# Attention and FFN block on one core: the value products of a step's two query blocks interleaved

## The chip, the cores and the metric

The kernel runs on one core of a Trainium2 chip. The metric is the device time of one execution in microseconds (us); lower is better. PE is TensorE, PEld its weight loads, DVE is VectorE, ACT is ScalarE, POOL is GpSimd, SP is SyncE, which here only issues DMAs.

## The reference, cut to what matters

One transformer layer on x of 1 x 2048 x 128 in fp32: layer norm, attention of 16 heads of 8 dimensions in a causal window of 32 tokens, a residual, layer norm, and a feed-forward part of 512 hidden units with GELU and a small weight update, again with a residual.

```python
scores = jnp.einsum('bhqd,bhkd->bhqk', q, k) * scale
allowed = (j <= i) & (i - j < WINDOW)          # WINDOW = 32
scores = jnp.where(allowed, scores, NEG_INF)
attn = jax.nn.softmax(scores, axis=-1)
out = jnp.einsum('bhqk,bhkd->bhqd', attn, v)   # the value products
...
x = x + attention(layernorm(x)); x = x + ffn(layernorm(x))
```

## The kernel before, in words

The 2048 tokens are cut into 8 chunks of 256, a chunk into 8 query blocks of 32 tokens (`WIN`). A block's queries see the keys of the block before and of their own, so each block has two windows `w` of 32 keys. The 16 heads form 4 groups (`NG`) of 4 (`GH`); a group's four heads stand one above the other in the 128 partitions, so one matmul serves four heads.

A **step** treats two blocks (`UB` = 2), so a chunk is 4 steps and the kernel has 32, numbered k here. Two chunks make a turn of 8 steps, and there are 4 turns, the middle ones in a hardware loop. The order on each engine is written out by hand in a function `step`; engines meet only at semaphores. On PE, step s does in this order:

1. `centre(s-1)` (L469): two bf16 matmuls of 512 columns that take the row maximum off the scores of step s-1, in PSUM.
2. `values(s-3)` (L490): the value products of step s-3.
3. `out_proj` (L536) in odd steps, `turn_att` (L532, a transpose of the attention output) in even ones.
4. In some steps pieces of a later chunk: `turn_x` (L416), `project` (L422, L423) and, behind the scores, `project_v` (L428).
5. `scores(s+1)` (L458): 16 bf16 matmuls, into the bank of scores that step s-1 used.

The bank of scores is double, so `scores(s+1)` waits until ACT has taken the exponential of step s-1 (`softmax_exp`, L684), which itself waits for `centre(s-1)`. DVE takes the maximum (L827), splits it (L833) and transposes the probabilities (L840), one step or more ahead of their use. All of ACT's copies share line L628 and are told apart by their tiles. ACT also copies the transposed attention output (attT), spreads the value rows out per head (V, 8 small copies at a time), copies xT for the next projection and in the last turn makes the token pairs of the FFN's weight update. Like every engine it works through its list in order.

In `values` each of a step's two blocks i has 4 groups x 2 windows = 8 fp32 products, each 32 stationary columns (the transposed probabilities) by 36 moving columns (the value rows of four heads and four columns of ones for the denominators). The result of block j stands in PSUM partitions 32q to 32q+31 with q = j mod 4, that is, in one of four 32-column tiles of the array. In a step the two blocks have q = 0 and 1, or q = 2 and 3. The two windows of a group are summed in PSUM (`start` at w = 0, `stop` at w = 1). The last product raises `pv_ps`, for which DVE and ACT wait. The program has 16 products in a step, and the trace shows each as two weight loads and two matmuls, as it does with every fp32 matmul: 32 matmul records in a step, 1024 in all.

After the last turn the FFN (`up` L513, `turn_x2` L499, `down` L611) runs with PE as the engine that never rests.

Of the kernel before, what the change touches and what calls it, by code (L numbers as in the profile page):

```python
# [26 lines left out]
P = 128  # L27
# [3 lines left out]
NG = HEADS // GH  # L31
WIN = 32
# [4 lines left out]
UB = BLOCKS // UNITS  # L37
# [13 lines left out]
def block_kernel(nc, x, Wq, bq, Wk, bk, Wv, bv, Wo, bo, W1, b1, W2, b2, scale, out):  # L51
# [10 lines left out]
    with ExitStack() as ctx:  # L62
# [112 lines left out]
        def ge(eng, s, value):  # L175

            if not isinstance(value, int) or value > 0:
                eng.wait_ge(s, value)
# [222 lines left out]
        def _(pe):  # L401
# [72 lines left out]
            def values(turn, s):  # L474
                k, b, u = SU * turn + s, s // UNITS, s % UNITS
                if u == 0:
                    c = 2 * turn + b
                    pe.wait_ge(v_done, c + 1)
                if isinstance(turn, int) and k == 0:
                    pe.wait_ge(wT_sb, 2)  # L480
                if s % 2 == 0:
                    ge(pe, att_done, (SU // 2) * turn + s // 2 - 1)
                pe.wait_ge(probsT_done, k + 1)
                o = bank_o[(s // 2) % 2]
                for i in range(UB):
                    j = UB * u + i
                    q = j % (P // WIN)
                    for g in range(NG):
                        for w in range(2):
                            mm = nc.tensor.matmul(o[q * WIN:(q + 1) * WIN, g * VC:(g + 1) * VC],  # L490
                                                  probsT[s % 2][:, i, g, w, :], V[b][:, j + w, g, :],
                                                  start=(w == 0), stop=(w == 1))
                mm.then_inc(pv_ps, 1)
# [44 lines left out]
            def step(turn, s, last):  # L538
# [7 lines left out]
                if not (first and s < 3) and s < SU + 3:  # L546
                    values(turn if s >= 3 else turn - 1, (s - 3) % SU)
# [463 lines left out]
```

## Time and profile before

| | |
|---|---|
| median of 3 runs | 165.35 us (164.3 to 165.49) |
| the profiled execution, first to last instruction | 162.8 us |
| mean granted TensorE clock | 0.979 |
| PE busy | 145.1 us, 89% of the span |
| PEld busy | 113.8 us, 70% |
| DVE busy | 99.5 us, 61% |
| ACT busy | 89.3 us, 55% |
| POOL busy | 51.0 us, 31% |
| `values` (L490), PE | 1024 matmuls, union of their records 36.8 us |
| `scores` (L458), PE | 512 matmuls, union 35.8 us |

The span is one execution seen by the profiler; the device time has some 2.5 us around it. Busy time of PE is a union of records whose ends are modelled: matmuls are pipelined, a record of L490 lasts 0.2 us while a new one starts every few hundredths, so for PE the distance between starts is what to read. "Granted clock" 1.00 is 2.4 GHz, 0.50 is 1.2 GHz.

### The profile page before, as it was taken

What the parts mean: (1) busy time and instruction counts of PE and PEld (TensorE: products, weight loads), DVE (VectorE), ACT (ScalarE), POOL (GpSimd) and SP (SyncE); (2) the same over time, 40 slices, a digit from 0 to 9 for tenths busy, and PEclk for the clock granted to TensorE, in tenths of its full rate; (3) what the DMA queues carried; (4) which work ended last, traced back from release to release, by engine and by line L of the source; (5) the groups of instructions that cost most, each with busy time, mean ns of one, the idle gap of its engine ahead of it and who ended that gap; (6) DMA issues with size and microseconds to landing.
All of it is one profiled execution on the core that took longest, in us unless ns stands there. A gap on an engine that the chain in (4) does not pass through costs nothing.

```text
span 162.8 us, 5053 instructions
## 1 busy us (share of the span) xinstructions
PE 145.1 (89%) x1923; PEld 113.8 (70%) x1923; DVE 99.5 (61%) x281; ACT 89.3 (55%) x256; POOL 51.0 (31%) x78
## 2 busy tenths in 40 slices
PE   0755298699999999999999999999799999999993
PEld 0423185578887887888788878788667665958792
DVE  6687956945576685695595597869665354221021
ACT  3354357558386577666677757529912567060600
POOL 6369578910060060051041030503600039800000
PEclk9999999659999999999999999999999999999999
DMA  1786897957044928618809908900000000020213
GB/s 50 219 215 243 202 366 168 330 168 178 0 151 167 240 97 268 188 61 297 195 4 332 212 0 306 230 19 0 4 0 4 0 2 4 0 64 0 64 45 88
DMA packets 27313, 21.10 MB, mean 130 GB/s; under 512 B 1304, under 2 KB 23071, under 8 KB 27295
## 3 DMA queue, kind: packets, MB, share of 16 engines
q1 hardware_dynamic: 27294, 20.85, 43.0%
q8 instruction: 12, 0.20, 0.5%
q14 instruction: 7, 0.05, 0.1%
HBM read 10.88 MB, written 9.96 MB: 128 GB/s over the span
## 4 chain that ended last, share of the span: by engine, by line
PE 80%; ACT 7%; DVE 5%; issue 2%; SPq 2%; DMA 1%; POOL 1%; DVEq 0%
PE bank_o L490 20%; PE bank_s L458 16%; PE bank_s L469 9%; PE bank_qk L611 4%; PE bank_s L513 4%; PE bank_w L536 3%; PE bank_v L611 3%; PE bank_o L513 3%; PE bank_qk L422 3%; ACT V L628 3%; PE bank_v L428 3%; PE bank_w L532 2%; PE bank_qk L423 2%; PE bank_t L416 2%; DMA x_sb<-in_L_attn_x_dram 1%
## 5 line engine op out<-in xcount | busy, mean ns | idle before, releaser
L490 PEld LDWEIGHTS bank_o<-V,probsT 128*32 128x32 f32 x1024 | 33.1, 114 | 15.1 <-issue 14.2
L458 PEld LDWEIGHTS bank_s<-KS,QS 128*128 128x128 bf16 x512 | 35.6, 166 | 4.5 <-ACT probs L684 3.9
L458 PE MATMUL bank_s<-KS,QS 128*128 128x64 bf16 x512 | 35.8, 225 | 2.3 <-ACT probs L684 2.2
L490 PE MATMUL bank_o<-V,probsT 128*32 128x36 f32 x1024 | 36.8, 201 | 0.0
L827 DVE TENSOR_REDUCE negmax<-bank_s 128x8 f32<-128x512 f32 x32 | 22.1, 690 | 22.9 <-PE bank_s L458 21.5
L684 ACT ACTIVATE probs<-bank_s 128x512 f32<-128x512 f32 x32 | 19.1, 598 | 22.4 <-PE bank_s L469 22.3
L628 ACT ACTIVATE V<-bank_v 32x64 f32<-32x64 f32 x128 | 27.5, 215 | 1.5
L840 DVE STREAM_TRANSPOSE probsT<-probs 128x512 f32<-128x512 f32 x32 | 22.5, 702 | 0.0
L285 POOL TENSOR_TENSOR q_parts<-rest,q_parts 128x256 bf16<-128x256 f32 x8 | 5.6, 705 | 53.7 <-ACT q_parts L628 53.7
L372 POOL TENSOR_TENSOR rstd<-var,half 128x4 f32<-128x4 f32 x4 | 4.1, 1020 | 28.6 <-DVE var L871 28.6
L469 PE MATMUL bank_s<-negmax,ident_bf 128*128 128x512 bf16 x32 | 12.6, 395 | 0.1
L469 PE MATMUL bank_s<-negmax_low,ident_bf 128*128 128x512 bf16 x32 | 12.6, 395 | 0.0
L628 ACT ACTIVATE attT<-bank_w,bias_cols 128x128 f32<-128x128 f32 x16 | 5.9, 369 | 11.4 <-PE bank_w L532 11.4
L833 DVE TENSOR_TENSOR negmax_low<-negmax 128x8 bf16<-128x8 f32 x32 | 11.3, 352 | 0.2
L416 PE MATMUL bank_t<-ident,xn 128*128 128x128 f32 x16 | 4.0, 342 | 7.0 <-DVE xn L800 7.0
L862 DVE TENSOR_TENSOR x<-bank_w,x_bo 128x128 f32<-128x128 f32 (+1 forms) x16 | 4.6, 286 | 9.1 <-PE bank_w L536 9.0
L628 ACT ACTIVATE q_parts<-bank_qk,bias_cols 128x256 bf16<-128x256 f32 x8 | 3.8, 475 | 10.4 <-PE bank_qk L423 10.4
L757 ACT ACTIVATE hidden<-bank_o,bias_cols 128x512 f32<-128x512 f32 x6 | 4.0, 687 | 8.7 <-PE bank_o L513 8.5
L416 PEld LDWEIGHTS bank_t<-ident,xn 128*128 128x128 f32 x16 | 2.1, 165 | 8.5 <-DVE xn L800 8.5
L270 POOL TENSOR_TENSOR rstd<-var,half 128x2 f32<-128x2 f32 (+2 forms) x4 | 6.0, 1493 | 6.1 <-DVE var L794 6.1
L422 PE MATMUL bank_qk<-xT,wq 128*128 128x256 f32 x16 | 6.7, 512 | 1.2 <-ACT xT L628 1.2
L611 PEld LDWEIGHTS bank_qk<-w2T,hidden 128*128 128x128 f32 x64 | 7.4, 192 | 0.5 <-issue 0.5
(109 smaller groups left out, 232.5 us busy)
## 6 DMA issues: line engine op xcount, KB each, us to landing
k_scr<-k_parts SPq DMA_DIRECT2D x8, 576.0 KB, 5.0
KS<-k_scr SPq DMA_DIRECT2D x8, 576.0 KB, 5.1
q_scr<-q_parts SPq DMA_DIRECT2D x8, 512.0 KB, 3.0
QS<-q_scr SPq DMA_DIRECT2D x32, 128.0 KB, 3.0
x_sb<-in_L_attn_x_dram SPq DMA_DIRECT2D x1, 768.0 KB, 5.3
out_dram<-y SPq DMA_DIRECT2D x3, 256.0 KB, 2.3
w<-in_L_ffn_W_dram SPq DMA_DIRECT2D x2, 256.0 KB, 5.4
x_sb<-in_L_attn_x_dram SPq DMA_DIRECT2D x2, 128.0 KB, 2.2
```

Of the source, the lines that this page charges most:

```text
L416: mm = nc.tensor.transpose(bank_t[:, t * P:(t + 1) * P], xn[b][:, t], ident[:])
L422: nc.tensor.matmul(bank_qk[:, 0:CHUNK], wq[:], xT[b][:], start=True, stop=True)
L458: mm = nc.tensor.matmul(dst, QS[b][:, o, g].rearrange("p h t -> p (h t)")[:, j::BLOCKS], KS[b][:, o, g, j * WIN:(j + 2) * WIN], start=(i = ...
L469: mm = nc.tensor.matmul(bank_s[s % 2][:].rearrange("p (a k) -> p a k", k=2 * WIN), ident_bf[:], part.unsqueeze(2).to_broadcast([P, UB * NG ...
L490: mm = nc.tensor.matmul(o[q * WIN:(q + 1) * WIN, g * VC:(g + 1) * VC], probsT[s % 2][:, i, g, w, :], V[b][:, j + w, g, :], start=(w == 0), ...
L513: nc.tensor.matmul(bank_h(f, c)[:], w1T[:, c * P:(c + 1) * P], x2T[f % 2][:], start=True, stop=True).then_inc(h_ps, 1)
L611: mm = nc.tensor.matmul(bank_y[:, t * D:(t + 1) * D], hidden[f % 2][:, c, t * P:(t + 1) * P], w2T[:, c], start=(c == 0), stop=(c == HC - 1))
L628: return nc.scalar.activation(dst, src, ACT.Identity, **kw)
L684: nc.scalar.activation(probs[s % 2][:], bank_s[s % 2][:], ACT.Exp, scale=float(HD) ** -0.5).then_inc(probs_done, 1)
L827: nc.vector.tensor_reduce(negmax[s % 2][:], bank_s[s % 2][:].rearrange("p (a k) -> p a k", k=2 * WIN), AX.X, ALU.max, negate=True).then_in ...
L833: nc.vector.tensor_tensor(negmax_low[s % 2][:], negmax[s % 2][:], high_half(negmax[s % 2]), ALU.subtract).then_inc(max_parts, 1)
L840: nc.vector.transpose(probsT[s % 2][:].rearrange("p i g w q -> p (i g w q)"), probs[s % 2][:]).then_inc(probsT_done, 1)
```

## The change

The three loops of `values` are put in another order. Before, block i is the outermost loop: all 8 products of the first block, then all 8 of the second. After, the block is the innermost: one product of the first block, one of the second, and so on. The products, their operands, the order of the two windows within a group and the last product with its signal are the same.

```diff
-                for i in range(UB):
-                    j = UB * u + i
-                    q = j % (P // WIN)
-                    for g in range(NG):
-                        for w in range(2):
+                for g in range(NG):
+                    for w in range(2):
+                        for i in range(UB):
+                            j = UB * u + i
+                            q = j % (P // WIN)
                             mm = nc.tensor.matmul(o[q * WIN:(q + 1) * WIN, g * VC:(g + 1) * VC],
                                                   probsT[s % 2][:, i, g, w, :], V[b][:, j + w, g, :],
                                                   start=(w == 0), stop=(w == 1))
```

Between engines nothing moves. PE's list in a step with a projection, from one `centre` to the next, reads so before and after alike; the 16 products of a step are one row, since they share their names and shapes:

```order
67 L469 MATMUL bank_s<-negmax,ident_bf 128x512
68 L469 MATMUL bank_s<-negmax_low,ident_bf 128x512
69 L178 ISA
70 L483 REGISTER_ALU
71 L490 MATMUL bank_o<-V,probsT 32x36 x16
72 L536 MATMUL bank_w<-wo,attT 128x128
73 L422 MATMUL bank_qk<-xT,wq 128x256
74 L423 MATMUL bank_qk<-xT,wk 128x256
75 L458 MATMUL bank_s<-KS,QS 128x64 x16
```

Within row 71 the order was eight products into tile q and then eight into tile q+1; now they alternate, which as matmul records is two, two, two.

## Rows read from the trace of the kernel before

**Rows 1.** The page: PE's share, and the chain that ended last, by line.

```profile
PE 145.1 (89%) x1923; PEld 113.8 (70%) x1923; DVE 99.5 (61%) x281; ACT 89.3 (55%) x256; POOL 51.0 (31%) x78
...
PE bank_o L490 20%; PE bank_s L458 16%; PE bank_s L469 9%; PE bank_qk L611 4%; PE bank_s L513 4%; PE bank_w L536 3%; PE bank_v L611 3%; PE bank_o L513 3%; PE bank_qk L422 3%; ACT V L628 3%; PE bank_v L428 3%; PE bank_w L532 2%; PE bank_qk L423 2%; PE bank_t L416 2%; DMA x_sb<-in_L_attn_x_dram 1%
```

**Rows 2.** Timeline of PE, one chunk: start us, length us, instruction, count.

```profile
61.95 1.12 PE L490 MATMUL bank_o<-V,probsT 128*32 128x36 f32 x32
63.00 0.33 PE L532 MATMUL bank_w<-ident,att 128*128 128x128 f32 x1
...
64.33 0.38 PE L469 MATMUL bank_s<-negmax,ident_bf 128*128 128x512 bf16 x1
...
65.91 0.49 PE L536 MATMUL bank_w<-wo,attT 128*128 128x128 f32 x2
66.24 0.60 PE L422 MATMUL bank_qk<-xT,wq 128*128 128x256 f32 x2
...
67.10 1.12 PE L458 MATMUL bank_s<-KS,QS 128*128 128x64 bf16 x16
...
69.80 1.10 PE L458 MATMUL bank_s<-KS,QS 128*128 128x64 bf16 x16
...
71.27 0.38 PE L469 MATMUL bank_s<-negmax,ident_bf 128*128 128x512 bf16 x1
```

**Rows 3.** Windows of L490 on PE: stretch, its length, busy, (matmuls), granted clock, DMA.

```profile
61.90:61.99 0.09, 0.04 (x1) 1.00 1.02 384
61.90:62.35 0.45, 0.40 (x12) 1.00 1.03 389
61.90:62.48 0.58, 0.53 (x19) 1.00 1.00 377
61.90:62.88 0.98, 0.93 (x32) 1.00 1.05 381
33.00:34.72 1.72, 1.67 (x32) 0.50 0.19 72
```

**Rows 4.** Timeline of ACT beside rows 2: start us, length us, [idle before <-releaser].

```profile
63.37 0.37 ACT L628 ACTIVATE attT<-bank_w,bias_cols 128x128 f32<-128x128 f32 x1 [0.72 <-PE bank_w L532]
63.76 1.82 ACT L628 ACTIVATE V<-bank_v 32x64 f32<-32x64 f32 x8
65.61 0.39 ACT L628 ACTIVATE xT<-bank_t 128x256 f32<-128x256 f32 x1
65.89 0.59 ACT L684 ACTIVATE probs<-bank_s 128x512 f32<-128x512 f32 x1
...
68.69 0.60 ACT L684 ACTIVATE probs<-bank_s 128x512 f32<-128x512 f32 x1 [0.54 <-PE bank_s L469]
```

**Rows 5.** Timeline of ACT in the last turn.

```profile
103.72 0.60 ACT L684 ACTIVATE probs<-bank_s 128x512 f32<-128x512 f32 x1
...
109.87 0.60 ACT L684 ACTIVATE probs<-bank_s 128x512 f32<-128x512 f32 x1 [2.19 <-PE bank_s L469]
...
117.29 0.61 ACT L684 ACTIVATE probs<-bank_s 128x512 f32<-128x512 f32 x1
```

**Rows 6.** Timeline of PE in the last turn.

```profile
104.37 1.15 PE L458 MATMUL bank_s<-KS,QS 128*128 128x64 bf16 x16
...
117.96 1.17 PE L458 MATMUL bank_s<-KS,QS 128*128 128x64 bf16 x16 [0.83 <-ACT probs L684]
```

**Rows 7.** Windows of PE: stretch, length, busy (matmuls), granted clock, DMA share, GB/s.

```profile
28.00:30.07 2.07, 1.38 (x18) 1.00 0.84 213
30.07:36.90 6.83, 6.18 (x63) 0.50 0.75 250
109.24:117.96 8.72, 7.83 (x141) 1.00 0.01 2
```

**Rows 8.** Timelines of DVE and PE: a transpose, and the values that read it.

```profile
69.94 0.70 DVE L840 STREAM_TRANSPOSE probsT<-probs 128x512 f32<-128x512 f32 x1
...
71.80 0.38 PE L490 MATMUL bank_o<-V,probsT 128*32 128x36 f32 x6
```

**Rows 9.** The page's group of the scores' loads: | busy, mean ns | idle before <-releaser.

```profile
L458 PEld LDWEIGHTS bank_s<-KS,QS 128*128 128x128 bf16 x512 | 35.6, 166 | 4.5 <-ACT probs L684 3.9
```

## The prediction, made before the changed kernel ran

> **What bounds the kernel now.** I read the page first: PE is busy for 89% of the span, DVE for 61%, ACT for 55%, and in the chain that ended last `values` (L490) holds 20%, more than any other line [rows 1]. A share is no proof, so next came PE's timeline over one chunk of four steps. The reader should see that its starts follow each other without an idle mark: centre, values, out projection or transpose, scores, again and again. From the centre at 64.33 to that of two steps later at 71.27 nothing waits [rows 2]. In such a stretch every tenth taken from PE's list is a tenth off the time, until another engine is late. Two such lengths of slack have to be found, and they come from ACT's timeline beside it [rows 4].
>
> **What values costs now.** It takes 1.05 us a step: its first matmul starts at 61.95, the next instruction at 63.00 [rows 2]. The windows split that [rows 3]. At full clock 12 matmuls start in the first 0.40 us, one each 33 ns, all in the first block's tile. Then 7 start within 0.13 us, one each 19 ns. The last 13 take 0.40 us again. The quick stretch is where the program passes from one tile to the other. I read it so: a tile takes a new fp32 matmul each 33 ns, whatever else goes on, and for a short while both tiles are at work at once, because the second tile's first records reach the array while the last ones of the first tile are still queued. If only one tile could work at a time, 32 matmuls at 33 ns would take 1.06 us, and they take 0.93. The change extends this double stretch over all 32 matmuls.
>
> **The new length.** Each tile has 16 matmuls, 15 distances of 33 ns = 0.49 us. The first distance in a step is longer: only one matmul has started by 61.99, 0.04 us after the first [rows 3]; I add 0.02 us. The second tile begins behind the first product, up to 0.04 us later. Sum 0.55 us. If instead the 19 ns of the quick stretch held throughout, it would be 32 x 19 ns = 0.60 us; if both tiles began together, 0.51 us. So the saving is 0.93 - 0.55 = **0.38 us a step**, with bounds 0.33 and 0.42. The stretch of 0.12 us between the last matmul of L490 and the next instruction, 1.05 less 0.93, stays: the change does not touch it. Neither loads nor matmuls are added, and nothing is waited for that was not waited for before.
>
> **What of it reaches the end.** 32 steps x 0.38 = 12.16 us of PE time. Four things are taken off or added.
>
> (a) Steps with a projection. ACT's list there is one unbroken row of work, started by PE's transpose at 63.00: attT at 63.37, eight V copies, xT from 65.61, which ends at 66.00. L422 needs xT and starts at 66.24 [rows 2, 4]. With about 0.04 us for the signal, PE has 0.20 us of slack. It would come 0.38 earlier, so 0.18 is lost. This happens at four steps (k = 8, 12, 16, 20): -0.72 us. The exponential behind xT ends at 66.48 and the scores start at 67.10, 0.62 later, so it is not late next.
>
> (b) The shortest distance of an ordinary step between the end of its exponential and the scores that overwrite its bank is 69.29 to 69.80 = 0.51 us [rows 2, 4]. Where ACT really is late the distance is 117.90 to 117.96 = 0.06 [rows 5, 6]. Slack 0.45, just over 0.38. I take off 0.03 for each of eight such steps: -0.24.
>
> (c) The last turn. The scores at 104.37 follow an exponential that ends at 104.32; ACT was late there already, so the values of that step give nothing. From 109.87 to 117.90 ACT works without rest at V copies, exponentials and token pairs; PE waits 0.83 us for it at 117.96 [rows 5, 6]. The values of three steps lie in that stretch and give nothing either. Four steps: -1.52.
>
> (d) The first values stand in the slow stretch, clock 0.50 from 30.07 to 36.90 [rows 7], where 32 matmuls take 1.67 us [rows 3]. By the proportion 0.55 to 0.93 they would take 0.99, so 0.68 is saved, 0.30 more than in another step. But the next ones then start before 36.90 and run partly at the low clock; I put that at 0.2 of the 0.3 and keep +0.1.
>
> Sum: 12.16 - 0.72 - 0.24 - 1.52 + 0.1 = **9.8 us**. A chunk in the middle goes from 12.7 us to 12.7 - 1.52 + 0.18 + 0.03 = 11.4. The profiled execution goes from 162.8 to 153.0. It had no unusual wait, and its 162.8 lies 2.55 under the median of 165.35; with the same distance the median becomes 155.6 us. At the bounds 0.33 and 0.42 the same sum gives 8.4 and 10.7 us (at 0.33 the losses are 0.56, 0 and 1.32), so 154.7 to 157.0.
>
> What else could be late: DVE's transposed probabilities are ready at 70.64 and PE takes them at 71.80 [rows 8], 1.16 us later, three times what a step shortens by, and DVE's list moves forward with PE's. The loads of the scores' weights wait 3.9 of their 4.5 us for ACT [rows 9], so the DMAs that bring queries and keys are ahead; I count nothing for them.
>
> **The rivals.**
>
> *The quick stretch draws on a stock.* The 7 starts in 0.13 us may be records that had piled up in front of the array, while a steady stream cannot be delivered so fast. All that the rows show as sustained is 33 ns from matmul to matmul. Half-way between that and 19 is 26 ns: 0.83 us a step, saving 0.10 to 0.15. Over 28 steps that is 2.8 to 4.2 us, and the time 161.8 us. Against it: PE's list is known long ahead in each step, so the stock should be refilled. Chance 0.13.
> The Trainium skill has a rule of this kind ("TensorE: Matmul & The Clock Gate", Wait — 56ns, not 53.3ns?): starts are never closer than about 25 ns, however few columns a matmul has. By it the 32 would take 0.78 us, 0.15 saved a step; the 19 ns of this trace are below that floor, but only for seven starts. The same page (Part 3, packing small matmuls) gives 2.38 times for three column tiles at 512 moving columns, which speaks for the forecast; no run shown here has that size.
>
> *The clock falls.* PE has more idle time after the change in the last turn: between 109.24 and 117.96 three values shorten by 1.1 us in all under a stretch whose length ACT sets. PE was busy for 7.83 of 8.72 us there and kept its clock; before the fall at 30.07 it was busy for 1.38 of 2.07 [rows 7]. After the change it would be 6.7 of 8.7, between the two. A fall as long as the one that starts at 30.07, 6.8 us, would cover two to three steps. In each the values would take some 0.4 us more, by the proportion of 1.67 to 0.93, and centre and the FFN's first products are lengthened alike: about 1 us a step, 2 to 3 us, 158 us. Chance 0.10.
>
> *Nothing changes.* The double stretch could depend on one tile's records being all handed over before the other's begin; with two records here and two there the array might take turns. Then 165.4 us. The 19 ns stretch, where records of both tiles start in turn, speaks against it. Chance 0.09.
>
> *Slower.* A tile's first product takes longer than its followers: the first distance is over 0.04 us where later ones are 33 ns. If every passage from tile to tile paid such a restart of 0.02 us and the tiles did not overlap, 15 passages cost 0.3 us a step and the lost quick stretch 0.13: 28 x 0.43 = +12 us, 177 us. It is decided at the point where the restart outweighs the overlap; a restart of 0.02 us with overlap costs next to nothing, since it passes beside the other tile's work. The one passage that each step has today shows no loss. Chance 0.05.
>
> **How the numbers follow.** Forecast 0.63, stock 0.13, clock 0.10, nothing 0.09, slower 0.05. A measurement of this kernel can tell about 1% from no change. The first three are all faster by over 1%: 0.86; within 1%: 0.09; slower: 0.05. The range reaches from a little under the forecast's own 154.7 to the stock's time: 154.3 to 161.8. It holds the first three cases.
>
> **What would show it.** In the changed profile L490's 32 matmuls should start within about 0.55 us, evenly, one each 17 ns, and the next instruction 0.12 later. L490's union on PE should fall by a third. L422 should wait for xT four times by about 0.2 us, and L458's waits for the exponential grow by about 1.5 us, most of it between 110 and 118. Steps of the middle turns should add up to 11.4 a chunk. An even 25 ns would make the stock right; a clock of 0.50 after 110 us the third; starts of 33 ns or more the last two.

## The result, and the profile after

The changed kernel takes 154.79 us (median of 4 runs, 154.03 to 155.87) against 164.82 us before (164.21 to 165.49, 4 runs of the same session). The ratio is 0.938, 95% interval 0.933 to 0.944: 10.0 us faster. A second series of runs of the same kernel, with the kernel before beside it, gave 154.21 against 164.73 us, ratio 0.937 (0.933 to 0.941). The profiled execution went from 162.8 to 152.2 us. The forecast was 155.6 us, with a forecast execution of 153.0.

Windows of L490 on PE in the changed kernel, for the step that answers to [rows 3]: stretch, its length, busy, (matmuls), granted clock, DMA. The last window is the first step, at half clock.

```profile
60.70:60.82 0.12, 0.08 (x4) 1.00 0.74 220
60.70:60.84 0.14, 0.10 (x6) 1.00 0.68 200
60.70:60.85 0.15, 0.11 (x6) 1.00 0.65 190
60.70:60.87 0.17, 0.13 (x8) 1.00 0.64 193
60.70:60.99 0.29, 0.25 (x15) 1.00 0.47 141
60.70:61.26 0.56, 0.52 (x32) 1.00 0.45 139
33.00:34.00 1.00, 0.95 (x32) 0.50 0.60 224
```

The first matmul of this step starts at 60.74 and the last one, the 32nd, 0.52 us later, where it was 0.93. Fifteen have started after 0.25 us and seventeen more in the next 0.27: on average one each 17 ns. They are not evenly spaced: in the records of this step they come in pairs, two starts 6 to 7 ns apart and one pair each 33 ns, as the jumps from 4 to 6 to 8 show. That is one start in each tile, and each tile keeps its 33 ns.

PE's timeline in the changed kernel over the chunk that answers to [rows 2]: start us, length us, instruction, count.

```profile
60.21 0.38 PE L469 MATMUL bank_s<-negmax,ident_bf 128*128 128x512 bf16 x1
60.43 0.38 PE L469 MATMUL bank_s<-negmax_low,ident_bf 128*128 128x512 bf16 x1
60.74 0.71 PE L490 MATMUL bank_o<-V,probsT 128*32 128x36 f32 x32
61.38 0.49 PE L536 MATMUL bank_w<-wo,attT 128*128 128x128 f32 x2
61.92 0.70 PE L422 MATMUL bank_qk<-xT,wq 128*128 128x256 f32 x2
62.46 0.59 PE L423 MATMUL bank_qk<-xT,wk 128*128 128x256 f32 x2
62.89 1.12 PE L458 MATMUL bank_s<-KS,QS 128*128 128x64 bf16 x16
63.85 0.38 PE L469 MATMUL bank_s<-negmax,ident_bf 128*128 128x512 bf16 x1
...
66.67 0.38 PE L469 MATMUL bank_s<-negmax,ident_bf 128*128 128x512 bf16 x1
...
69.11 0.38 PE L469 MATMUL bank_s<-negmax,ident_bf 128*128 128x512 bf16 x1
...
71.61 0.38 PE L469 MATMUL bank_s<-negmax,ident_bf 128*128 128x512 bf16 x1
```

From values to the next instruction are 0.64 us, 60.74 to 61.38, where there were 1.05. The chunk from 60.21 to 71.61 takes 11.40 us, as forecast; it took 12.70. Its four steps take 3.64, 2.82, 2.44 and 2.50 us, where the steps with the same work took 3.73, 3.21, 2.85 and 2.91. Three of them gave 0.39 to 0.41 us. The one with the projection gave 0.09.

ACT's timeline beside it, which answers to [rows 4]:

```profile
59.25 0.37 ACT L628 ACTIVATE attT<-bank_w,bias_cols 128x128 f32<-128x128 f32 x1 [0.25 <-PE bank_w L532]
59.65 1.82 ACT L628 ACTIVATE V<-bank_v 32x64 f32<-32x64 f32 x8
61.48 0.39 ACT L628 ACTIVATE xT<-bank_t 128x256 f32<-128x256 f32 x1
```

xT ends at 61.87 and L422 starts at 61.92: now it waits for xT.

The page of the changed kernel, groups of L458 and L490: | busy, mean ns | idle before, releaser.

```profile
L458 PE MATMUL bank_s<-KS,QS 128*128 128x64 bf16 x512 | 35.9, 226 | 3.8 <-ACT probs L684 3.8
...
L490 PE MATMUL bank_o<-V,probsT 128*32 128x36 f32 x1024 | 23.3, 201 | 0.0
```

L490's records cover 23.3 us, 36.8 before. A record lasts 201 ns as before: no product became faster, they stand beside each other.

**Where the time went.** Starts of the centre of a few steps in the two profiles, and what lies between:

| stretch | before | after | saved |
|---|---|---|---|
| start to centre 0 | 25.64 | 26.33 | -0.69 |
| centre 0 to 8 | 25.98 | 22.44 | 3.54 |
| centre 8 to 20, three chunks | 38.13 | 34.31 | 3.82 |
| centre 20 to 22 | 6.93 | 6.45 | 0.48 |
| centre 22 to 26 | 12.56 | 11.33 | 1.23 |
| centre 26 to 29 | 11.53 | 11.37 | 0.16 |
| centre 29 to 31 | 5.90 | 5.07 | 0.83 |
| centre 31 to the end | 36.13 | 34.90 | 1.23 |

### The profile page after: what moved, and what is told of

Read it like the earlier page. It is cut to its first block, busy times and chain, and to the rows that moved or that the text cites. A ratio compares the mean times of both kernels' runs of the same rounds, so it can differ in the third digit from the quotient of the medians.

```text
span 152.2 us, 5053 instructions
## 1 busy us (share of the span) xinstructions
PE 132.2 (87%) x1923; PEld 100.4 (66%) x1923; DVE 99.2 (65%) x281; ACT 89.6 (59%) x256; POOL 51.4 (34%) x78
## 4 chain that ended last, share of the span: by engine, by line
PE 72%; ACT 13%; DVE 5%; issue 3%; SPq 2%; DMA 2%; POOL 1%; ACTq 0%; DVEq 0%
PE bank_s L458 16%; PE bank_o L490 10%; PE bank_s L469 8%; ACT V L628 7%; PE bank_qk L611 5%; PE bank_s L513 5%; PE bank_qk L422 4%; PE bank_v L611 4%; PE bank_o L513 3%; PE bank_qk L423 3%; PE bank_v L428 3%; PE bank_w L532 2%; PE bank_w L536 2%; ACT probs L684 2%; ACT xT L628 2%
## 5 line engine op out<-in xcount | busy, mean ns | idle before, releaser
L458 PE MATMUL bank_s<-KS,QS 128*128 128x64 bf16 x512 | 35.9, 226 | 3.8 <-ACT probs L684 3.8
L458 PEld LDWEIGHTS bank_s<-KS,QS 128*128 128x128 bf16 x512 | 34.9, 164 | 6.0 <-ACT probs L684 5.3
L490 PEld LDWEIGHTS bank_o<-V,probsT 128*32 128x32 f32 x1024 | 19.6, 114 | 14.8 <-issue 12.7
L490 PE MATMUL bank_o<-V,probsT 128*32 128x36 f32 x1024 | 23.3, 201 | 0.0
L833 DVE TENSOR_TENSOR negmax_low<-negmax 128x8 bf16<-128x8 f32 x32 | 8.7, 273 | 0.2
L422 PE MATMUL bank_qk<-xT,wq 128*128 128x256 f32 x16 | 7.2, 537 | 1.6 <-ACT xT L628 1.2
L513 PE MATMUL bank_s<-x2T,w1T 128*128 128x512 f32 x16 | 7.7, 593 | 0.0
```

What stands on the lines that cost most here:

```text
L422: nc.tensor.matmul(bank_qk[:, 0:CHUNK], wq[:], xT[b][:], start=True, stop=True)
L458: mm = nc.tensor.matmul(dst, QS[b][:, o, g].rearrange("p h t -> p (h t)")[:, j::BLOCKS], KS[b][:, o, g, j * WIN:(j + 2) * WIN], start=(i = ...
L513: nc.tensor.matmul(bank_h(f, c)[:], w1T[:, c * P:(c + 1) * P], x2T[f % 2][:], start=True, stop=True).then_inc(h_ps, 1)
L833: nc.vector.tensor_tensor(negmax_low[s % 2][:], negmax[s % 2][:], high_half(negmax[s % 2]), ALU.subtract).then_inc(max_parts, 1)
```

## The experiments

The theory: a 32-column tile takes a new fp32 matmul of 36 columns each 33 ns, two tiles do so side by side, and a tile's matmuls must be handed over early enough, since they are handed over in the order of the program and few can wait in front of a busy tile. Behind values, ACT keeps part of the gain. Rivals: alternation of the blocks or of the operands helps by itself, whatever the tile; only a fixed stretch overlaps at a passage; every step gives all that values saves.

### One tile only

Both blocks' products go to the first block's tile, two and two. The second block's rows of the attention output are left out.

```diff
+                for g in range(NG):
+                    for i in range(UB):
+                        for w in range(2):
                             j = UB * u + i
-                            q = j % (P // WIN)
-                            ... matmul(o[q * WIN:(q + 1) * WIN, g * VC:(g + 1) * VC],
+                            q = (UB * u) % (P // WIN)
+                            n = i * NG + g
+                            ... matmul(o[q * WIN:(q + 1) * WIN, n * VC:(n + 1) * VC],
```

> The value products alternate between the two blocks, two products of the one, two of the other, but both blocks write the same 32-column tile (the second block beside the first in other columns of the bank), so the second block's rows of the attention output are not computed. Theory (two tiles work at once, one tile takes a matmul each 33 ns): 32 matmuls start over 31 x 33 ns = 1.02 to 1.05 us, a little more than the 0.93 of before, because the one overlap at the passage is gone too; time about 0.1 x 28 = 3 us over the kernel before, 167 to 169 us. Rival (the order alone, or alternating between blocks, is what helps, not the tile): 0.52 us and about 155 us.

The windows of its values line for one step:

```profile
64.30:65.37 1.07, 1.03 (x32) 1.00 0.35 67
```

The starts cover 1.03 us, 33 ns apart from the third to the last. The time is 167.02 us, ratio 1.011 (1.004 to 1.018), 2.0 us over before. It is the tile that counts, not the order of the blocks; the next run is its counterpart. A middle chunk takes 13.12 us, 0.42 more than before, which is four steps of 0.10: what the one passage in each step was worth.

### Two products of a block, then two of the other

The loop over i stands between those over g and w. As the trace counts, that is four matmuls in a row for one tile.

```diff
                 for g in range(NG):
-                    for w in range(2):
-                        for i in range(UB):
+                    for i in range(UB):
+                        for w in range(2):
```

> Both windows of a group for one block, then both for the other: four matmuls in a tile before the passage to the next. Theory (records are handed over in order, and up to three matmuls may wait in front of a busy tile while the next tile's are handed over): A's four are handed over at once, so B starts with A; 0.52 us from first to last as in the changed kernel, and the same time, ratio to it 1.00. Rival (the overlap needs alternation product by product): between 0.6 and 0.8 us, 157 to 162 us.

Windows of L490 for one step:

```profile
61.60:61.96 0.36, 0.27 (x15) 1.00 0.11 32
61.60:62.23 0.63, 0.54 (x32) 1.00 0.09 29
```

0.54 us from the first to the last start, 0.02 more than in the changed kernel, and 155.38 us, ratio 0.936 (0.929 to 0.943). A strict alternation is not needed. With the first experiment this pair has the same order of products and differs in the tile alone: 1.03 against 0.54 us.

### Four products, then four

```diff
+                for h in range(2):
+                    for i in range(UB):
+                        for g, w in ((2 * h, 0), (2 * h, 1), (2 * h + 1, 0), (2 * h + 1, 1)):
```

> Four products (eight matmuls) of a block, then four of the other, twice. Theory (three matmuls may wait in front of a busy tile): the second tile starts when the fifth matmul of the first starts, 0.15 us in; the first tile's next eight start about 0.31 us in, the second's about 0.46, and the last starts at 0.69 to 0.71 us. That is 0.23 us under before, nearly all of it kept where PE bounds: about 28 x 0.23 = 6.3 us, 158.5 us. Rival (only the last matmuls at a passage overlap by a fixed sum of 0.1 us, or the queue ahead is much deeper than three): 0.93 - 2 x 0.1 = 0.73 us by the first, 0.52 us by the second.

Windows of L490 for one step, all from the same start:

```profile
63.40:63.60 0.20, 0.14 (x4) 1.00 0.38 120
63.40:63.62 0.22, 0.17 (x6) 1.00 0.46 123
63.40:63.80 0.40, 0.34 (x15) 1.00 0.54 160
63.40:64.18 0.78, 0.72 (x32) 1.00 0.69 204
```

Four matmuls stand alone for 0.14 us, then two start within 0.02: the fifth of the first tile and the first of the second. The last starts at 0.72 us; the theory said 0.69 to 0.71, the fixed overlap 0.73, the deep queue 0.52. The deep queue is out. The other two can't be parted here, since three matmuls of 33 ns are the same 0.1 us as the fixed overlap. What this run shows is the place of the second tile's start: it came when the fifth of eight started, so three matmuls were still waiting in front of the busy tile. The same number fits before, where the second tile starts with the 13th of 16 and the quick stretch begins after 12 [rows 3], and the run before this one, where a tile has only four in a row and only 0.02 us is lost.

The kernel before parts them, since its first values run at half clock. Windows of its L490 there:

```profile
33.00:33.78 0.78, 0.72 (x12) 0.50 0.27 103
33.00:33.80 0.80, 0.74 (x14) 0.50 0.27 103
```

One tile takes a matmul each 60 ns at this clock, and 31 of these distances are 1.86 us, where 1.65 to 1.67 were measured: 0.2 us overlap, twice as long as at full clock. The second tile again starts with the 13th matmul. So what is fixed is the number of waiting matmuls and not a time. Whether the three are counted for one tile or for the whole array, and whether weight loads count, no run here shows.

The time is 159.9 us, ratio 0.967 (0.962 to 0.972), 5.2 us under before where 6.3 were expected: values saved 0.21 us a step, not 0.23, and of the 0.84 us of a middle chunk 0.71 arrived (11.99 us).

### The new order in the last turn alone

```diff
+                late = isinstance(turn, int) and turn == SUPER - 1
+                order = ([(i, g, w) for g in range(NG) for w in range(2) for i in range(UB)] if late else
+                         [(i, g, w) for i in range(UB) for g in range(NG) for w in range(2)])
```

> Interleaved in the last turn alone (8 of 32 steps), the order of before in the others. Theory (ACT sets the length of the stretch with the token pairs, three of these eight give nothing): 5 x 0.41 = 2.0 us under before, 162.7 us. Rival (every step gives what it is shortened by): 8 x 0.41 = 3.3 us, 161.5 us; then the losses taken off in the forecast were no losses. The step lengths between centre 26 and centre 29 tell it apart too: 11.5 us as before by the theory, 10.3 by the rival.

PE's timeline of this kernel in the stretch of the token pairs:

```profile
109.59 0.38 PE L469 MATMUL bank_s<-negmax,ident_bf 128*128 128x512 bf16 x1
...
114.39 1.18 PE L458 MATMUL bank_s<-KS,QS 128*128 128x64 bf16 x16 [0.86 <-ACT probs L685]
...
118.14 1.17 PE L458 MATMUL bank_s<-KS,QS 128*128 128x64 bf16 x16 [1.07 <-ACT probs L685]
...
120.94 0.38 PE L469 MATMUL bank_s<-negmax,ident_bf 128*128 128x512 bf16 x1
```

From centre 26 to centre 29 are 11.35 us, against 11.53 before and 11.37 in the changed kernel. The theory said 11.5, the rival 10.3. The three values in it are 1.2 us shorter, and 0.2 us of that arrives; the rest became the waits of 0.86 and 1.07 for ACT's exponential, where before there was one of 0.83 [rows 6]. The profiled execution is 1.9 us shorter than before (160.9). The time is 162.61 us, ratio 0.983 (0.979 to 0.988), against 165.06 us for the kernel before in the same session. The ratio's interval stands for 2.0 to 3.5 us: faster, but it does not part the theory's 2.0 from the rival's 3.3. The stretch from centre 26 to 29 does.

### xT copied before the V copies

The wait for xT was tested by moving ACT's copy of xT from the next step to the place ahead of the eight V copies.

```diff
                 if s < SU:
                     c = 2 * turn + b
-                    if p1 and u == 1:
-                        copy_xT(c + 2, b)
...
+                if s < SU and p1 and u == 0:
+                    copy_xT(2 * turn + b + 2, b)
```

> The changed kernel, and ACT copies xT before the eight V copies of the step instead of behind them, so that it is ready for the projection early. Theory (in the changed kernel each of four projections waits for xT, 0.21 us, and then shows 0.10 us of weight load that was hidden before): 4 x 0.31 = 1.2 us under the changed kernel, 153.6 us; the step with the projection 3.33 instead of 3.64 us, the chunk 11.1 instead of 11.4. Rival (the exponential behind the V copies holds the scores up in its turn, or the wait only moves): the chunk stays at 11.4 and the time at 154.8.

PE's timeline in the step with the projection:

```profile
60.09 0.38 PE L469 MATMUL bank_s<-negmax,ident_bf 128*128 128x512 bf16 x1
...
61.26 0.49 PE L536 MATMUL bank_w<-wo,attT 128*128 128x128 f32 x2
61.58 0.60 PE L422 MATMUL bank_qk<-xT,wq 128*128 128x256 f32 x2
62.02 0.59 PE L423 MATMUL bank_qk<-xT,wk 128*128 128x256 f32 x2
62.45 1.12 PE L458 MATMUL bank_s<-KS,QS 128*128 128x64 bf16 x16
63.41 0.38 PE L469 MATMUL bank_s<-negmax,ident_bf 128*128 128x512 bf16 x1
```

L422 starts 0.32 us after L536, not 0.54, and L423 0.44 us after L422, not 0.54. The step takes 3.32 us for 3.64 and the chunk 11.08 for 11.40. So the loss at the projection had two parts: the wait, 0.22, and 0.10 of L422's weight load that the wait had laid bare. The time is 153.84 us, ratio 0.933 (0.929 to 0.937). Its interval overlaps that of the changed kernel; the profile shows the gain, the times alone would not prove it. The rival is out as well: the exponential now ends at 62.23, and the scores behind the projection start at 62.45 without a wait.

### Four tiles

The values of two steps are done together in every second step, product by product over all four tiles.

```diff
+                        for s2, i in ((s - 1, 0), (s - 1, 1), (s, 0), (s, 1)):
+                            j = UB * (s2 % UNITS) + i
...
-                if not (first and s < 3) and s < SU + 3:
+                if not (first and s < 3) and s < SU + 3 and s % 2 == 0:
                     values(turn if s >= 3 else turn - 1, (s - 3) % SU)
```

> The values of two steps are done together in every second step, product by product over all four 32-column tiles. Theory (each tile takes a matmul each 33 ns by itself, and records are handed over fast enough): 64 matmuls start within 0.54 us, one each 8 ns. The steps without values are then set by the exponential (scores no earlier than 1.29 us after the centre) and by the ACT chain before the projection, so a chunk loses only 0.2 us (11.2), the tail after the last centre 1.3 us: about 3 us in all, 151.8 us. Rival (the array is handed a matmul each 16 ns at most, which the changed kernel just reaches): 64 matmuls in 1.03 us, the same sum of values as in the changed kernel, and 154 to 156 us.

Windows of its values line on PE for one pair of steps:

```profile
57.85:57.99 0.14, 0.08 (x8) 1.00 0.86 336
57.85:58.48 0.63, 0.57 (x64) 1.00 1.00 384
```

At the array the theory holds: 64 matmuls in 0.57 us, 9 ns each on average, four tiles side by side. The kernel gains nothing by it. The time is 155.53 us, ratio 0.945 (0.940 to 0.950), where 151.8 was expected. A middle chunk takes 11.52 us, not 11.2. Of its two steps without values the one with the projection takes 3.63 us, 0.90 of it a wait for xT, and the other 2.29, since it waits for the exponential (0.47 us in PE's timeline below). The steps with both values take 2.65 and 2.96; there the transpose L532 starts 0.70 and 0.83 us after the start of values, where it starts 0.64 us after it with two tiles.

```profile
66.52 0.38 PE L469 MATMUL bank_s<-negmax,ident_bf 128*128 128x512 bf16 x1
...
67.81 1.17 PE L458 MATMUL bank_s<-KS,QS 128*128 128x64 bf16 x16 [0.47 <-ACT probs L684]
```

In the last turn the clock fell, as in the forecast's second rival. Windows of all engines, busy time of PE, PEld, DVE, ACT and POOL in this order, then the granted clock:

```profile
100.00:108.44 8.44, 5.81 (x115) 4.49 (x113) 6.24 (x20) 6.94 (x28) 4.32 (x4) 1.00 0.00 0
108.44:115.27 6.83, 6.06 (x57) 2.98 (x60) 1.69 (x6) 1.11 (x3) 0.00 (x0) 0.50 0.01 2
```

PE was busy for 5.81 of 8.44 us up to 108.44, and then the clock stood at 0.50 for 6.83 us. From centre 26 to 29 are 13.13 us, 1.8 more than in the changed kernel, where the stretch that answers to it keeps its clock (the changed kernel's window, same columns):

```profile
100.85:109.42 8.57, 6.60 (x142) 4.82 (x139) 6.96 (x22) 7.66 (x29) 4.33 (x4) 1.00 0.01 2
```

### Four tiles and the early xT

This is the kernel of the last section with ACT's copy moved as in the one before.

> Both: four tiles and the early copy of xT. Theory: the projection no longer waits, the scores behind it wait for the exponential instead, 0.47 us earlier than without: 4 x 0.47 = 1.9 us under e6_four_tiles, 149.9 us; chunk 10.7. Rival (four tiles bring nothing at the array): no better than e5_xt_first, 153.6.

154.5 us, ratio 0.936 (0.931 to 0.940). A middle chunk takes 11.04 us, 0.04 less than with two tiles and the early xT: four tiles are worth nothing in the loop. Both numbers expected by the theory, 149.9 and 10.7, were missed. They stood on the 151.8 and 11.2 that the kernel before it was expected to take. The difference that the theory named came in the loop: 11.52 less 11.04 is 0.48 us a chunk, and the scores behind the projection now wait 0.51 us for the exponential. From centre 26 to 29 are 12.70 us, again with a fall of the clock, at 110.8. It also fell at 97.15, for 3.4 us, and before that PE had been busy for more than in the stretch above where the changed kernel kept its clock (window of PE alone):

```profile
88.72:97.15 8.43, 6.80 (x132) 1.00 0.57 189
```

So PE's busy time over some 8 us does not say by itself when the clock falls.

### The changed kernel again, and the last two steps joined

> The changed kernel once more, unchanged, so that its time and e5's and e9's stand beside more runs. Theory: ratio 0.938 to before, 154.8 us. The stretch of the low clock near 30 us came and went with lengths of 0, 3.4 and 6.8 us in the profiles so far; if that stretch and not the change were behind the surplus over the forecast, the steps from centre 0 to centre 8 take 23 to 24 us in this profile where that stretch is 6.8 us long, and 22.4 where it is 3.4.

154.21 us, ratio 0.937 (0.933 to 0.941). The low clock near 30 us lasted 3.4 us in this profile, and centre 0 to 8 took 22.39 us, as expected for that length. The other half of the expectation, a length of 6.8 us with this kernel, was not met with, and so not tested here.

The other kernel takes xT early and joins the values of the last two steps over four tiles, where no exponential is waited for any more.

```diff
+                pair = isinstance(turn, int) and turn == SUPER - 1 and s == SU - 1
+                steps = ((s - 1, 0), (s - 1, 1), (s, 0), (s, 1)) if pair else ((s, 0), (s, 1))
```

> e5 (xT copied early), and the values of the last two steps done together over all four column tiles, where no exponential is waited for any more. Theory: one values of 0.52 us and one passage in and out of it (0.09 and 0.13 us) fall away: 0.7 us under e5, 153.1 us; from the last centre to the end 34.2 instead of 34.9 us. Rival (the joint values come later than the first of the two did, and the transposes behind them wait): 34.9 us, 153.8.

Its timeline of PE near the end of the last turn (L492 is its values line):

```profile
118.62 0.39 PE L539 MATMUL bank_w<-wo,attT 128*128 128x128 f32 x2
118.84 1.02 PE L516 MATMUL bank_s<-x2T,w1T 128*128 128x512 f32 x2
119.80 0.77 PE L492 MATMUL bank_o<-V,probsT 128*32 128x36 f32 x64
120.50 0.33 PE L535 MATMUL bank_w<-ident,att 128*128 128x128 f32 x1
```

From the last centre to the end are 34.11 us for 34.90. 152.66 us, ratio 0.927 (0.922 to 0.931): the fastest of all, and clear of the changed kernel's interval of the same session (0.933 to 0.941), though not of that of the early xT alone.

## Why the prediction was right, point by point

**What bounds it.** PE's list, as read from [rows 2]: the three steps of the middle chunk without a projection gave 0.39 to 0.41 us each for 0.41 saved in values.

**The new length.** Forecast 0.55, measured 0.52 us; the saving 0.41, not 0.38. The surplus in the term was the 0.04 us for the second tile's late beginning: in the records it begins 7 ns behind the first, not behind the first product. The reading of the quick stretch in [rows 3], both tiles at work at once, was shown by the pair of kernels that differ in the tile alone, 1.03 against 0.54 us. The forecast named no depth; the run with four and four and the half clock of before gave it: three matmuls may wait.

**(a) The projection.** Forecast a loss of 0.18 us, measured 0.32 (3.73 less 0.41 is 3.32, and the step takes 3.64). The mechanism was right, the size was not: the wait is 0.22 because values became shorter than forecast, and 0.10 is L422's weight load. Before, that load ran beside the instruction ahead: it started at 66.13, 0.11 us before its matmul. Behind the wait both start at 61.92. The early copy of xT gave the 0.32 back in full. In the chunk this error and that of the length cancel: 4 x 0.03 more saved, 0.14 more lost. The forecast of 11.4 us was right by two errors, which is luck. Over all four projections the loss is 1.4 us, twice the forecast's 0.72: these steps took 14.90 us together and take 14.65, where 4 x 0.41 were saved in values. With the early xT they take 13.24.

**(b) The exponential of an ordinary step.** Forecast 0.03, measured 0.02 (3.21 to 2.82 with 0.41 saved).

**(c) The last turn.** Forecast that four values give nothing. Between centre 26 and 29, where three of them stand, 0.16 of 1.2 us arrived, and the run with the new order in the last turn alone shows the same. From centre 22 to 26 stand four, and 1.23 us is three of them. The fourth is the step that the forecast named: it took 3.13 us and takes 3.07, and its scores, which before started just behind the exponential, now wait for it.

```profile
96.38 1.16 PE L458 MATMUL bank_s<-KS,QS 128*128 128x64 bf16 x16 [0.42 <-ACT probs L684]
```

This is where the gain stayed behind: under ACT's row of copies, exponentials and pairs. PE's waits for the exponential in front of L458 are 2.2 us in sum before and 3.8 after; the forecast said 1.5 more.

**(d) The slow stretch.** The forecast's weakest term. Forecast for centre 0 to 8, with six values: 6 x 0.38 + 0.1 = 2.4 us. Measured 3.54. But the low clock lasted 6.83 us before [rows 7] and 3.41 here:

```profile
28.00:32.52 4.52, 3.16 (x37) 2.41 (x36) 2.94 (x5) 2.88 (x11) 4.52 (x6) 1.00 0.92 277
32.52:35.93 3.41, 3.41 (x52) 2.17 (x50) 2.00 (x3) 2.40 (x10) 0.81 (x1) 0.50 0.44 161
```

Three kernels with the new pace of values had a stretch of 6.8 us there: two products of a block in turn (e2_runs_of_2), the early xT (e5_xt_first) and the joined last steps (e9_tail_pair). They took 23.31, 23.52 and 23.12 us, 2.5 to 2.9 less than before. So about 1 us of the 3.54 is luck of the profile and not of the change. The time from the start to centre 0 scatters too, between 25.5 and 26.4 us over all profiles; that luck went the other way, by 0.7 us.

The timed runs scatter with the clock as well. The kernel before has 33 runs on record with their granted clock: the median is 165.73 us at 0.948 (11 runs), 165.01 at 0.958 (5), 164.64 at 0.979 (13) and 164.10 at 0.989 (4). Runs at nearly the same clock are the better comparison: the changed kernel has 154.30 us at 0.978 (6 runs) and 153.94 at 0.988 to 0.989 (2 runs). That is 10.3 and 10.2 us less, so the gain of 10.0 in the medians is not made by the clock.

**The rivals.** The stock: 17 ns sustained over a step's 32 matmuls rules it out, and 9 ns over 64 with four tiles even more. Both are also below the Trainium skill's floor ("TensorE: Matmul & The Clock Gate", Wait — 56ns, not 53.3ns?), by which starts are never closer than about 25 ns. In this case that floor can be one for a single tile at most, where 33 ns were measured; here the measurement decides. Starts in two different tiles are 6 to 7 ns apart, a little over the 4 ns that the same page (Part 3, packing small matmuls) gives from tile to tile. The clock: in both profiles of the changed kernel it held in the last turn, with PE busy for 6.60 of 8.57 us. It fell there in both kernels with four tiles, in the first of them after 5.81 of 8.44 us, and in no other profile. The longest idle time of PE in front of these two falls was 1.9 us; in the changed kernel's stretch it is 1.1. That more idle time brings the fall is likely by this, but not shown: no run changed the idle time alone, and the fall at 97.15 came after a busier stretch. "Nothing changes" and "slower" fell with 0.52 us.

**The sum.** Forecast 9.8 us, measured 10.0 in time and 10.6 in the profiles. The 10.6 hold about 1 us of (d)'s luck, less the 0.7 us before centre 0, where the change touches nothing. The forecast's own sum with what was measured is 32 x 0.41 = 13.1, less 1.4 for (a), 0.1 for (b) and 1.5 for (c), and 0.3 more for the first values (1.65 to 0.92 us at half clock): 10.4 us, beside 10.2 and 10.3 at like clock. So 9.8 came near by a saving that was sized too small and a loss at the projection that was sized too small. Two slips in the arithmetic changed little. At the lower bound of 0.33 the sum gives 8.8 us and not 8.4, so 156.6 us and not 157.0. And 2.55 us, the "some 2.5 us" around the span in the section on the time before, are no distance between an execution and its own time: in each of the runs on record the time is 1.7 to 1.8 us over that run's own span. The profiled execution before was simply a faster one than the median. With 1.8 the forecast execution of 153.0 us gives 154.8 us, beside the 154.79 measured. That it agrees to the tenth is luck: the execution took 152.2.

## What to carry to other kernels

When small matmuls go to different column tiles, write the program so that no more than four matmuls in a row (two fp32 products) go to the same tile. A loop over tiles outermost gave only 0.1 us of overlap here, where alternation gave 0.5. A profile shows the chance before anything is changed: look for the short stretch where starts come at double pace, at a passage from tile to tile. Price the gain by the slack of the engine that feeds the next instruction, and add the weight load that a new wait lays bare; beyond that slack a faster array buys only idle time. In both kernels with four tiles, which had more of it than the changed one, the clock fell in the last turn.

## What the runs showed of the hardware that was not expected

- Three matmuls may wait in front of a busy column tile while the next tile's are handed over: the second tile started with the 5th of 8 and with the 13th of 16, the latter at full and at half clock.
- Four column tiles, fp32 products with 32 stationary and 36 moving columns, run side by side at 9 ns a matmul (64 in 0.57 us), 3.6 times the pace of one tile (32 in 1.03 us).
- The scores' matmuls (bf16, 64 columns) start mostly 60 to 64 ns apart, in one step after another; the shorter values change nothing in that: 0.94 us from scores to the next centre before (60.48 to 61.42) and 0.94 after (59.27 to 60.21).
- The low clock near 30 us came with lengths of 0 (one tile), 3.4 (the changed kernel, twice), 6.8 and 10.2 us (four tiles with the early xT) in kernels that differ little or not at all up to its start. One kernel's runs scatter too: the mean granted clock of the kernel before lies between 0.948 and 0.989. One profile's length of it is no property of a kernel.
